# Heads of a four-layer graph network: block transposes on VectorE and sixteen 32x32 products side by side in place of full transposes and column-group products on TensorE, with a new order of stages

## The reference, cut to what matters

```python
q = heads(x @ Wq)
k = heads(x @ Wk)
v = heads(x @ Wv)
scores = jnp.einsum('bhnd,bhmd->bhnm', q, k) / sqrt_dk
scores = jnp.where(mask, scores, -jnp.inf)
attn = jax.nn.softmax(scores, axis=-1)
out = jnp.einsum('bhnm,bhmd->bhnd', attn, v)
out = out.transpose(0, 2, 1, 3).reshape(b, n, d)
return jax.nn.relu(out) @ Wo
```

## Time and profile before

| | |
|---|---|
| three runs, us | 3774.29, 3777.41, 3780.37 |
| median, us | 3777.41 |
| profiled execution, its span from first to last instruction, us | 3773.6 |
| share of the span: PE, PEld, DVE, ACT, POOL | 88%, 68%, 65%, 58%, 20% |
| records of PE and of PEld | 18,240 each |
| packets and bytes of all transfers | 39,858, 40.24 MB |
| mean granted TensorE clock | 0.969 |

### The profile page before, as it was taken

How to read it: one execution, slowest core, us unless ns; L and a number is a source line. 1 busy time by engine, 2 the same in 40 slices (tenths; PEclk the granted TensorE clock), 3 DMA queues, 4 the chain that set the end, 5 groups by cost and what they waited for, 6 DMA issues and landing times.

```text
span 3773.6 us, 60010 instructions
## 1 busy us (share of the span) xinstructions
PE 3307.7 (88%) x18240; PEld 2566.8 (68%) x18240; DVE 2461.5 (65%) x7151; ACT 2196.3 (58%) x4349; POOL 773.1 (20%) x1052
## 2 busy tenths in 40 slices
PE   6689989898999899989998899889989898999866
PEld 4577766766667677666766677677766766667653
DVE  3466676666757666676666767666676666766654
ACT  2256556665565756656665565756656665565623
POOL 1212122121311222121121211222121121211210
PEclk8899999999999999999999999999999999999989
DMA  5000000000000000000000000000000000000000
GB/s 138 1 1 12 7 12 7 7 7 7 12 7 6 7 7 12 8 12 7 7 7 7 12 7 6 7 7 12 7 12 7 1 12 7 12 7 1 1 6 6
DMA packets 39858, 40.24 MB, mean 11 GB/s; under 512 B 7264, under 2 KB 38240, under 8 KB 39520
## 3 DMA queue, kind: packets, MB, share of 16 engines
q1 hardware_dynamic: 31072, 27.68, 2.5%
q0 software_dynamic: 8448, 8.39, 1.5%
HBM read 36.07 MB, written 8.39 MB: 12 GB/s over the span
## 4 chain that ended last, share of the span: by engine, by line
PE 49%; issue 23%; DVE 12%; ACT 12%; POOL 3%; DVEq 0%; DMA 0%; POOLq 0%; ACTq 0%; SPq 0%
PE acc L1210 11%; PE work L1234 9%; PE acc L1248 7%; PE acc L1314 3%; PE work L1151 3%; ACT PT L1044 3%; PE acc L1283 3%; PE acc L1295 2%; POOL rstd L515 2%; PE work L1122 2%; PE work L1263 2%; PE work L1195 2%; ACT L1044 2%; DVE T L697 2%; PE acc L1343 2%
## 5 line engine op out<-in xcount | busy, mean ns | idle before, releaser
L1234 PE MATMUL work<-XT,w_sb 128*128 128x256 f32 x3072 | 732.7, 384 | 36.6 <-DVE XT L821 15.0
L515 POOL TENSOR_TENSOR rstd<-var_eps,minus_half 128x2 f32<-128x2 f32 x320 | 225.2, 704 | 2601.2 <-DVE var_eps L773 2601.0
L1248 PE MATMUL acc<-w_sb,gT 128*128 128x256 f32 x3072 | 724.7, 383 | 0.0
L1234 PEld LDWEIGHTS work<-XT,w_sb 128*128 128x128 f32 x3072 | 557.7, 190 | 168.0 <-ACT gT L1026 35.4
L1248 PEld LDWEIGHTS acc<-w_sb,gT 128*128 128x128 f32 x3072 | 575.7, 192 | 95.7 <-issue 22.8
L1026 ACT ACTIVATE gT<-work,b_sb 128x256 f32<-128x256 f32 x768 | 342.3, 472 | 209.1 <-PE work L1234 201.6
L1210 PE MATMUL acc<-X,PT 128*128 128x256 f32 x1536 | 378.0, 402 | 24.7 <-ACT PT L994 24.1
L1210 PEld LDWEIGHTS acc<-X,PT 128*128 128x128 f32 x1536 | 305.0, 202 | 98.0 <-issue 31.1
L1026 ACT ACT_TABLE_LOAD x198 | 254.0, 1283 | 3.5
L757 DVE COPY PT<-work 128x512 f32<-128x512 f32 x160 | 109.6, 685 | 222.9 <-PE work L1195 221.2
L764 DVE BATCH_NORM_STATS2 stats<-R 128x6 f32<-128x256 f32 x640 | 240.9, 418 | 11.0
(11 more groups left out here) (155 smaller groups left out, 5955.3 us busy)
## 6 DMA issues: line engine op xcount, KB each, us to landing
HX<-in_x SPq DMA_DIRECT2D x16, 512.0 KB, 3.8
pos<-in_adj POOLq DMA_DIRECT2D x16, 512.0 KB, 5.7
out<-X SPq DMA_DIRECT2D x32, 256.0 KB, 2.1
w_sb<-in_L_gnn_W SPq DMA_DIRECT2D x6, 1024.0 KB, 8.6
g_sb<-in_L_gnn_g SPq DMA_DIRECT2D x6, 128.0 KB, 6.5
awr_sb<-in_L_gnn_attn_w SPq DMA_DIRECT2D x2, 256.0 KB, 7.8
c_sb<-in_L_gnn_beta SPq DMA_DIRECT2D x3, 128.0 KB, 4.3
PT<-in_L_gnn_b SPq DMA_DIRECT2D x3, 128.0 KB, 5.8
```

Source lines behind the costliest of these rows:

```text
L515: pool.tensor_tensor(rstd[s][:, half_rows(half)], var_eps[s][:, half_rows(half)], minus_half[:], ALU.pow)\
L1234: last = pe.matmul(u.bank[:, 0:HN], w1_sb[:, l, c, f * P:(f + 1) * P], XT[s][:, c, half * HN:(half + 1) * HN], start=(c == 0), stop=(c == ...
L1248: last = pe.matmul(acc[s][half][:, i, :], gT[s][:, f, i * P:(i + 1) * P], w2_sb[:, l, f, :], start=(f == 0 and i == 0), stop=(f == FC - 1) ...
```

## The change

- `uT` is gone from TensorE, ACT and DVE. Instead DVE transposes the 32x32 blocks inside each head tile (`bt`, two tiles a stage), from `score_tile` to `turned_tiles`, which lie in PT2, gT of the slot, and PT of the slot. `score_tile` is now a set of four tiles in T instead of a ring of eight.
- In a turned tile, partition group a holds the keys m whose position in their group of 128 lies in block a. So the values are spread to fit: SP (stages rp0, rp1) issues 16 transfers each, from 32 partitions of V to 32 partitions of HP. HP is one buffer that holds HX and pos1, which were two.
- `pv` m, now m = 0 and 1: 16 blocks b of 32 keys' columns by four row groups a (one bank each) by four column groups r, 256 products of 32 rows x 32 columns with 128 moving elements. All four banks are filled at once. `pc0` on ACT copies the four banks of m = 0 in four pieces, hn1 on DVE those of m = 1. The turned tiles of the second half (bt8) may be written only when pv0 is done, and rp1 starts then too.
- x and adj of the slot's next batch are loaded when pv1 is done.
- rden rows stand in the q and k buffers instead of T, rb1 is copied whole by ACT, and proj waits for the whole of hn1.
- HALF is new.

The diff, cut to its core:

```diff
-    GROUPS = 2 * DC
+    NB = N // DK
...
-        ("ending", "L3", "sq0 sr0"), ("middle", "L1.0", "xa1"), ("middle", "L1.1", "bc zs0 mx0"),
-        ("ending", "L3", "v1"), ("middle", "L1.1", "zs1 exp0 mx1"), ("ending", "L3", "qk1"),
-        ("middle", "L1.1", "exp1 pT0"), ("ending", "L3", "ex0"), ("middle", "L1.1", "pT1"),
-        ("ending", "L3", "ex1 sq1"), ("middle", "L1.1", "agg0"),
-        ("ending", "L3", "ex2 ex3 sr1 uT0 ex4 uT1 ex5 uT2 ex6 uT3"), ("middle", "L1.1", "pT2 pT3 sum0"),
...
+        ("middle", "L1.1", "ha0"), ("ending", "L3", "ex12 sq4 ex13 ex14 ex15 sr4"),
+        ("middle", "L1.1", "f200 f110 f201 f111"),
+        ("ending", "L3", "rr0 ex16 ex17 ex18 pc0 rp1 bt8 ex19 pv0 ex20 bt9 sq5 ex21 sr5 ex22"),
+        ("middle", "L1.1", "f202"), ("ending", "L3", "ex23 bt10"), ("middle", "L1.1", "f112 f203"),
+        ("ending", "L3", "ex24 bt11"), ("middle", "L1.1", "xsum0"), ("ending", "L3", "sq6 ex25 ex26 ex27"),
+        ("middle", "L1.1", "xnorm0"), ("ending", "L3", "sr6"), ("middle", "L1.1", "ha1"), ("middle", "L1.2", "sx0"),
+        ("middle", "L1.1", "f113 f210 f211"), ("ending", "L3", "bt12 bt13 sq7"), ("middle", "L1.1", "f212"),
+        ("ending", "L3", "sr7"), ("middle", "L1.1", "f213 xsum1"), ("ending", "L3", "ex28 ex29 ex30 ex31 rr1"),
+        ("middle", "L1.1", "xa0"), ("ending", "L3", "load rt0 rt1 rb0 rb1"), ("middle", "L1.2", "bc"),
+        ("ending", "L3", "pv1"), ("middle", "L1.1", "xa1"), ("ending", "L3", "bt14"), ("middle", "L1.1", "xnorm1"),
+        ("ending", "L3", "bt15 store0 store1"), ("middle", "L1.2", "sx1"), ("ending", "L3", "hn0"),
+        ("middle", "L1.2", "mx0"), ("ending", "L3", "hn1"), ("middle", "L1.2", "zs0 zs1 exp0 pT0 exp1 mx1 pT1"),
+        ("ending", "L3", "ysum0 proj0 proj1 ysum1"), ("middle", "L1.2", "pT2 pT3"), ("starting", "L0", "masks"),
...
-        HX = pair("HX", [P, NT, D])
+        HP = pair("HP", [P, 2 * NT * D])
+        HX = [HP[s][:, 0:NT * D].rearrange("p (t d) -> p t d", d=D) for s in range(SLOTS)]
...
-            place = n % (2 * NT)
-            return (T[s] if place < NT else PT[s])[:, place % NT, :]
+            return T[s][:, n % HPC, :]
+
+        def turned_tiles(s, r):
+
+            if r < 2:
+                return PT2[:].rearrange("p r a b -> p (r a b)").rearrange("p (r t n) -> p r t n", r=2, t=NT)[:, r]
+            return gT[s][:].rearrange("p f n -> p (f n)").rearrange("p (t n) -> p t n", n=N) if r == 2 else PT[s]
+
+        def values_of_blocks(s):
+
+            return HP[s][:].rearrange("p (t g d) -> p t g d", t=NT, g=HPC)
...
+            def spread_values(m):
+                def stage(s, it, key):
+
+                    if m == 0:
+                        for t in tiles(1):
+                            use = Use(s, it, "v1 L3", t % HT)
+                            sp.wait_ge(use.evacuated, use.turn + 1)
+                            hold(sp, "sync")
+                    else:
+                        for place in range(HPC):
+                            use = HeadUse(s, it, place, f"outputs {m - 1}")
+                            sp.wait_ge(use.filled, use.filled_at)
+                            hold(sp, "sync")
+                    for g in range(HPC):
+                        for a in range(HPC):
+                            sp.dma_start(values_of_blocks(s)[a * DK:(a + 1) * DK, :, g, :],
+                                         V[s][g * DK:(g + 1) * DK, :, m * P:(m + 1) * P]).then_inc(spread.sems[s], 16)
+                return stage
...
+            def blocks_turned(q, part):
                 m, half, i = QUADS[q]
 
                 def stage(s, it, key):
+                    if m and half * HT + i == 0 and part == 0:
+                        for place in range(HPC):
+                            use = HeadUse(s, it, place, f"outputs {m - 1}")
+                            dve.wait_ge(use.filled, use.filled_at)
+                    for r in range(2 * part, 2 * part + 2):
+                        n = HPC * q + r
+                        dve.wait_ge(exp_done.sems[s], exp_done.value(it, "heads", n))
+                        dve.transpose(turned_tiles(s, r)[:, half * HT + i, :], score_tile(s, n)).then_inc(turned.sems[s], 1)
                 return stage
...
+            def head_outputs(m):
+                def stage(s, it, key):
+                    pe.wait_ge(spread.sems[s], spread.value(it, f"m{m}", 16 * HPC * HPC - 1))
+                    pe.wait_ge(turned.sems[s], turned.value(it, "heads", (m + 1) * NK // DC - 1))
+                    places = [HeadUse(s, it, a, f"outputs {m}") for a in range(HPC)]
+                    for use in places:
+                        pe.wait_ge(use.evacuated, use.free)
+                    hold(pe, "tensor")
+                    for b in range(NB):
+                        for a, use in enumerate(places):
+                            rows = slice(a * DK, (a + 1) * DK)
+                            for r in range(HPC):
+                                last = pe.matmul(use.bank[r * DK:(r + 1) * DK, 0:P],
+                                                 values_of_blocks(s)[rows, b // HPC, b % HPC, r * DK:(r + 1) * DK],
+                                                 turned_tiles(s, r)[rows, :, b * DK:(b + 1) * DK],
+                                                 start=(b == 0), stop=(b == NB - 1), skip_group_check=True)
+                            if b == NB - 1:
+                                last.then_inc(use.filled, 1)
                 return stage
```

In the loads, SP's and POOL's waits for `kept` and `max_done` become waits for the four banks of the last outputs:

```diff
-                sp.wait_ge(kept.sems[s], kept.value(it, "L2", NT - 1))
-                hold(sp, "sync")
+                for place in range(HPC):
+                    use = HeadUse(s, it, place, f"outputs {DC - 1}")
+                    sp.wait_ge(use.filled, use.filled_at)
+                    hold(sp, "sync")
```

More of the change, by code:

```diff
@@ L210, in build @@
         pos0 = pair("pos0", [P, NT, N], BF16)
-        pos1 = pair("pos1", [P, NT, N], BF16)
+        pos1 = [HP[s][:, NT * D:2 * NT * D].bitcast(BF16).rearrange("p (t n) -> p t n", n=N) for s in range(SLOTS)]
         s12 = pair("s12", [P, NT, 2])
@@ L280, in build @@
         uses += [("xT0 L3", DC), ("v0 L3", HT), ("xT1 L3", DC), ("q L3", 1), ("k L3", 1), ("scores 0", 2), ("v1 L3", HT), ("q L3", 1), ("k L3", 1)]
[L281 to L283 removed]
+        for q in range(1, NQ):
+            uses += [(f"outputs {q // (NQ // DC) - 1}", 2)] if q % (NQ // DC) == 1 and q > 1 else []
+            uses += [(f"scores {q}", 2)]
+        uses += [("rden 1", 2), (f"outputs {DC - 1}", 2)]
         turn = Events(None, uses)
@@ L323, in build @@
         exp_done = signal("exp_done", [(k, NT) for k in ATT] + [("heads", NK)])
+        spread = signal("spread", [(f"m{m}", 16 * HPC * HPC) for m in range(DC)])
+        turned = signal("turned", [("heads", NK)])
         kept = signal("kept", [("L2", NT)])
@@ L865, in stage @@
                 def stage(s, it, key):
+                    if q:
+                        dve.wait_ge(turned.sems[s], turned.value(it, "heads", HPC * (q - 1) + 2 * part + 1))
+                    if part == 0:
+                        last = HeadUse(s, it, HPC - 1, f"scores {q}")
+                        dve.wait_ge(last.filled, last.filled_at)
+                    if q or part == 0:
+                        hold(dve)
                     for r in range(2 * part, 2 * part + 2):
```

124 lines of the change are left out of this document (36 added, 88 removed), and 83 rows, old and new, of the table HALF.

## The result

| | before | after |
|---|---|---|
| median, us (4 runs each) | 3778.89 | 3878.11 |
| lowest to highest, us | 3774.29 to 3784.23 | 3876.62 to 3882.84 |
| span of the profiled execution, us | 3773.6 | 3875.7 |
| mean granted clock | 0.969 | 0.902 |

A forecast was written before the change was run, and what follows sets the result against it. TensorE was taken as the bound. Per batch, 18 us of output stages less 21.6 removed gave -3.6, plus 1.8 given back: -1.8, times 16 = -29, so 3748 us; range 3590 to 3955.

The forecast's parts named there:

- three of 3.0, since the first is there when the stage begins: 9 us, twice 18: TensorE's two output stages: each waits for three of its four instruction packets at 3.0 us, 18 us a batch together.
- 10.8 us a stage: Output stage length from which TensorE's added work outweighs the 21.6 us a batch removed, making a slower result decisive.
- The lower one, 3.9 us at 7.5 ns a record: Lower end for an output stage: pure array time with sixteen small products side by side, 512 records in 3.9 us.
- Rival B: Output stages keep the array's pace, 3.9 us each; TensorE -13.8, period -9 us a batch, 3633 us; chance 0.21.
- The upper end for the feed, 12.6 us: Output stage limited by instruction fetch: four packets at up to 3.15 us each, 12.6 us a stage.
- Rival C: Output stages: every instruction has a time to issue, 15 ns, 15.4 us a stage; +11.2 a batch, 3956 us; chance 0.16.
- Rival E: Output stages: row and column groups don't combine, four products run at once; 15.4 us a stage, 3924 us; chance 0.11.
- A microsecond saved on it is worth nearly a microsecond: TensorE ends most waits, so its saved time becomes kernel time nearly one for one, until VectorE is the later.
- The stand before bt8 was put at 8 us: VectorE waits most of the first output stage before the second half's block transposes may overwrite the turned tiles: 8 us.
- I give half of TensorE's gain back: Allowance for new waits of VectorE and ScalarE around the first output stage and the single score-tile set: 1.8 us a batch.
- Rival D: VectorE becomes the bound in the heads, through bt8 and the single score-tile set; +6.7 a batch, 3885 us; chance 0.18.
- Under 0.95: Granted clock below 0.95 as a sign of a wrong forecast; a thinly used array after each output stage might cost +2.

The follow-up runs named there:

- twelve_blocks: Changed kernel with twelve rounds of sixteen products in an output stage in place of sixteen, same columns in three quarters of the instructions; 3765.9 us.
- short_moving: Changed kernel with output products moving 32 columns in place of 128, same number of instructions; 3844.9 us.
- wide_blocks: Changed kernel with eight blocks of 256 moving elements in place of sixteen of 128 in both output stages, half the instructions; 3623.5 us.
- holes_filled: Changed kernel with three idle identity products of 384 columns put ahead of each hole of the output stages; 3901.3 us.
- spaced_first: Changed kernel with the first output stage cut into four parts and feed-forward stages f201, f111, f202 between them; 3862.4 us.

## Why the prediction was wrong

**The output stage.** This step failed, in its size: "three of 3.0, since the first is there when the stage begins: 9 us, twice 18". Measured: 13.0 and 13.2, together 8.2 us more, and the whole miss of the period is 9.5 (234.6 against 225.1); at the 1.02 to 1.27 us of time that a microsecond of stage was worth, the 8.2 make 8.4 to 10.4. The mechanism was the named one, packets of 256 instructions and clumps with holes "<-issue". Two things were off. I took the eating of a packet, 1 us, as lying inside the 3.0 of its bringing; the trace has 1.6 us of eating and then 2.1 of standing, 3.7 in all. And I gave one packet free; there are three such spacings and a part of a fourth. twelve_blocks tried the forecast's own size and gave 3766. My point of decision for a slower result, 10.8 us a stage, is close to the 10 that the three block counts give.

**The bounds.** The lower one, 3.9 us at 7.5 ns a record, was too low: at full clock and without holes 207 records took 2.73 us, 13 ns each, 6.7 us a stage. Rival B was never to be had. The upper end for the feed, 12.6 us, was passed by half a microsecond: it was four packets of 3.15 us, a stall and a bringing each, with nothing for the eating; measured are three and a half of 3.7. Rival C asked for evenly spaced records; there are none, and the Trainium skill's floors (Runtime: NRT & Kernel Launch, Instruction fetch mechanics; TensorE: Matmul & The Clock Gate, Back-to-back issue gap) do not show: 20 cycles an instruction (17 ns at 1.2 GHz, an estimate from that page's figure) stand against 13 ns for a product record and its load together, and 25 ns for a small matmul, which the page gives for up to 64 columns, against 8 ns for a record of 32 columns and its load (0.27 us for 32 in short_moving). So C had the direction, but not the reason. Rival E is excluded by the same rate.

**TensorE as the bound.** "A microsecond saved on it is worth nearly a microsecond" was read from a busy share of 88 to 91%, and it did not hold at the two places tried: nothing came back at either in the kernel before, and in the changed kernel half of it at one and none at the other. That the forecast came out within 1% for stages near its 9 us (twelve_blocks) is in part luck, for the sum priced all of TensorE's work alike. The 21.6 us of transposes and outputs that went were also waits of VectorE and ScalarE, and what each of the two was worth no run tells apart. Stage time, on the other hand, was worth 1.0 to 1.3; I put that down to next to nothing running beside it (ACT's 4.46 us in the first of the four stretches above), which is a reading of the rows and was not tried by itself.

**VectorE.** Its transposes were priced right (0.61 us apart forecast, 0.60 in the trace). The stand before bt8 was put at 8 us and is 14.1, since the stage is longer. "I give half of TensorE's gain back" had no row behind it. Its busy time grew by 14.2 us a batch (2687.9 less 2461.5, by 16), not 10.8; the difference is told below. Rival D had the right place, the block of VectorE around bt8, and 3885 against 3878; but its own sum, a stretch that VectorE lengthens by itself, is not what the runs show: half the block transposes gone gave 3.1 us a batch, the four packets of two stages gone (wide_blocks) 15.9. VectorE's block is a partner, not the cause alone.

**ScalarE, transfers, loads.** Costed at 0 (1 us for xa1 at most), and no run or row speaks against it. GpSimd stands 17.3 us before its load in 14 of the 16 batches, and xa1 behind it (1574.6 to 1578.3) is done before agg0 needs it at 1580.45, as reckoned.

**The clock.** Under 0.95 was listed as a sign of being wrong, at +2 us a stage. It is 0.902, and holes_filled puts it at 2.5 us a batch behind the first stage and nothing behind the second. Inside a stage little of the +2 is seen: the second one, at 0.50 throughout, takes 13.2 us and the first, at a mean of 0.79 in the stage shown, 13.0.

## What to carry to other kernels

Count instructions, not only columns. Where a stage of many small products runs faster than its code arrives, its price is the number of packets times nearly the whole of bringing and eating one, here 3.7 us for 256 instructions. Cutting the columns to a quarter took 1.2 us off a stage of 13, cutting the instructions to a half took 7. Before taking a microsecond of an engine as a microsecond of the kernel, leave that engine's work out once and time it; a busy share of 90% said nothing here. A stage at which other engines must stand was paid for here at its full length and a little more, and feed-forward work put into its holes gave back only a quarter of what it saved TensorE, since VectorE's chain stayed as long.

## What was not expected of the hardware

**Code arrives late, not only slowly.** TensorE's next packet is on its way only when the last one is nearly eaten at full clock: in the stage above the first two packets start 0.8 and 0.5 us before their holes do (1517.64, 1521.12). The Trainium skill (Runtime: NRT & Kernel Launch, Instruction fetch mechanics) has the next page brought while the current one runs, at a cost "mostly hidden"; for 256 instructions eaten in 1.6 us the trace shows 2.1 us of standing, and the measurement decides. The holes nearly went where a stage had two packets of longer products (wide_blocks) and went where full-size products stood at the boundary (spaced_first, holes_filled). At half clock, where 128 records last 2.6 us, the packet starts 0.7 to 1.4 us before the hole (second stage above), and TensorE still stands for 1.0 to 1.6 us from start to start.

**Sixteen small products do run together.** 32 records with 128 columns take 0.41 us, and 0.64 at 0.50 of the clock. Half of the 0.41 is the part that does not shrink with the columns (short_moving).

**VectorE beside GpSimd.** One record of the normalization on VectorE takes 0.41 us alone and 0.81 (medians over the changed kernel's trace) while GpSimd multiplies or adds beside it, as at 1541.02 (VectorE's timeline, then GpSimd's):

```profile
1541.02 1.61 DVE L799 TENSOR_SCALAR HP<-R,mean_var,rstd 128x256 f32<-128x256 f32 x2
```

```profile
1540.26 1.42 POOL L542 TENSOR_TENSOR R<-HP,g_sb 128x256 f32<-128x256 f32 x2
1541.75 1.46 POOL L546 TENSOR_TENSOR R<-R,c_sb 128x256 f32<-128x256 f32 x2
```

The new order brings the two together more often: the mean of the group went from 413 to 585 ns, 3.4 us of VectorE a batch, and that is the part of its growth that I had not counted. Whether it costs time was not tried by itself.
